# 16-bit tables for TensorE's register loads in a graph network kernel

## What is computed

```python
for l in range(3):
    X = einsum('ne,ref->rnf', out, weights[l])
    msg = X[edge_type, src] + biases[l][edge_type]
    hidden = segment_sum(msg, dest, N)      # dest = first row of edge_index
    out = relu(hidden) if l < 2 else hidden
x = layernorm(x + out)
# attention: alpha = cosine(x[row], x[col]) * beta, softmax over the edges of a row,
# out = segment_sum(alpha * x[col], row);   x = layernorm(x + out)
```

## Time and profile before

| | us |
|---|---|
| median of three runs | 5249.69 |
| the three runs | 5255.31, 5249.69, 5236.56 |
| span of the profiled execution | 4129.8 |
| PE busy | 2926.3 |
| DVE busy | 2722.0 |
| POOL busy | 2587.4 |

### The profile page before, as it was taken

The page is one execution under the profiler, slowest core; times in us unless marked ns, Lnnn a source line. Parts: engine busy times, 40 slices in busy tenths (PEclk is TensorE's granted clock), DMA queues, the critical chain, the costliest instruction groups (busy, mean ns, idle before and its releaser), DMA issues.

```text
span 4129.8 us, 59123 instructions
## 1 busy us (share of the span) xinstructions
PE 2926.3 (71%) x14075; PEld 1889.2 (46%) x14077; DVE 2722.0 (66%) x9148; ACT 820.3 (20%) x1995; POOL 2587.4 (63%) x2738
## 2 busy tenths in 40 slices
PE   7899966776777677676777667776766444446998
PEld 4455544444444444444444444444444333334776
DVE  9988875666666666666666656666665333336999
ACT  2588801001100100100100010000010000003665
POOL 0677767777777770777777777437777777771000
PEclk9899988888888888888888888888887555557999
DMA  4100013322332333332233233243224111113654
GB/s 154 51 2 2 6 41 78 85 74 73 86 78 73 82 80 150 77 85 74 73 86 78 72 82 82 53 180 81 73 73 91 53 53 53 53 53 100 191 187 142
DMA packets 373888, 336.56 MB, mean 81 GB/s; under 512 B 262034, under 2 KB 326090, under 8 KB 373448
## 3 DMA queue, kind: packets, MB, share of 16 engines
q0 software_dynamic: 87104, 158.80, 15.6%
q1 hardware_dynamic: 83112, 113.25, 8.1%
q10 hardware_dynamic: 203360, 60.73, 6.1%
HBM read 225.44 MB, written 107.13 MB: 81 GB/s over the span
## 4 chain that ended last, share of the span: by engine, by line
PE 36%; DVE 34%; issue 12%; POOL 11%; ACT 4%; DMA 2%; DVEq 0%; SPq 0%; POOLq 0%; ACTq 0%
PE ps L1067 12%; POOL region L935 11%; PE ps L1012 9%; DVE region L605 9%; DVE region L539 9%; DVE region L540 7%; PE ps L1056 7%; DVE oh L534 3%; PE ps L1128 2%; PE ps L1098 2%; PE ps L1156 2%; DMA region<-x_of_type,arrays 2%; ACT ps L1214 2%; ACT region L1225 2%; DVE region L378 1%
## 5 line engine op out<-in xcount | busy, mean ns | idle before, releaser
L935 POOL DMA_INDIRECT region<-x_of_type,arrays x2418 | 2286.8, 946 | 945.6 <-issue 718.3
L1067 PE MATMUL ps<-region 128*128 128x510 f16 x4200 | 1455.6, 437 | 551.2 <-issue 297.5
L534 DVE TENSOR_SCALAR oh<-iota_w,arrays 128x102 f32<-128x102 f32 x2528 | 734.2, 292 | 1303.9 <-PE ps L1056 1265.6
L1056 PE MATMUL ps<-region,oh 128*102 x5040 | 1142.9, 332 | 552.6 <-SPq L837 357.6
L1056 PEld LDWEIGHTS ps<-region,oh 128*102 128x102 f32 x5040 | 967.8, 212 | 1129.6 <-issue 870.8
L1067 PEld LDWEIGHTS ps<-region 128*128 128x128 f16 x4200 | 443.1, 108 | 665.6 <-issue 620.3
L605 DVE TENSOR_TENSOR region<-region,ps 102x128 f32 x2520 | 713.3, 283 | 3.4 <-issue 3.1
L1225 ACT COPY region<-ps 128x510 f32<-128x510 f32 x155 | 89.8, 579 | 2374.6 <-PE ps L1067 2374.2
L539 DVE TENSOR_SCALAR region<-ps,arrays 128x640 f16<-128x640 f16 x844 | 459.3, 544 | 0.0
L918 POOL DMA_INDIRECT scattered_edges<-region x304 | 296.5, 975 | 208.1 <-DVE shiftcol L442 110.4
L540 DVE TENSOR_SCALAR region<-ps,arrays 128x510 f16<-128x510 f16 x844 | 399.5, 473 | 0.0
(11 more groups left out here) (217 smaller groups left out, 1441.7 us busy)
## 6 DMA issues: line engine op xcount, KB each, us to landing
edge_counts<-region ACTq DMA_DIRECT2D x155, 255.0 KB
region<-x_of_type,arrays POOLq DMA_INDIRECT x2418, 2.5
arrays<-edge_counts SPq DMA_DIRECT2D x40, 960.0 KB, 5.0
x_of_type<-region SPq DMA_DIRECT2D x50, 576.0 KB, 2.8
edge_absent<-region ACTq DMA_DIRECT2D x155, 127.5 KB
region<-edge_absent SPq DMA_DIRECT2D x40, 480.0 KB, 4.0
x_of_type<-x0st SPq DMA_DIRECT2D x51, 192.0 KB, 1.8
scattered_edges<-region POOLq DMA_INDIRECT x304, 2.1
```

The lines of the kernel that those rows point to most:

```text
L534: ins = nc_.tensor_scalar(oh[:, t % U, 0:RB], iota_r, rowf[:, t % NT:t % NT + 1], None, ALU.is_equal)
L935: pool.indirect_dma_start(out=grow[:, t % GR * D:(t % GR + 1) * D], out_offset=None, in_=xt, in_offset=bass.IndirectOffsetOnAxis(ap=gix[:, ...
L1056: mm = pe.matmul(ps[0:RB, 6 + n % 2, t * D:(t + 1) * D], oh[:, u % U, 0:RB], grow[:, bass.ds(at[u % PAIRS], D)], start=True, stop=True)
L1067: mm = pe.matmul(ps[:, c, 0:CW], cl[:, q % CR, c * P:(c + 1) * P], cr[:, q % CR, :], start=False, stop=False, skip_group_check=True)
```

## The change

- The three tables are 16-bit integers without sign, all in `x0st`, in rows of ROW16 = 16 numbers (32 bytes). A row of `steps_of` belongs to PAIRS = 8 slots: 8 places (`slot_at`) and 2 due tiles (`tile_due`). A row of `banks_due` belongs to one turn's 10 cells and holds CG times (block number + 1), what was `b7`'s value plus CG - 1. `b7` is no longer used for it, nor is its padding set.
- PE loads a row of 8 + 2 numbers every 8 slots with one load (`steps_at`), where it had one load of 8 and one of 2.
- PE loads 10 bank numbers at the start of a turn with cells (`banks_at`), where it had two loads of 5 within the turn.
- Both declare why their values stay in bounds, so no comparisons and assertions follow.
- The wait for `s_cz` takes the register as it is, without adding CG - 1.

```diff
--- before.py
+++ after.py
@@ -22,6 +22,7 @@
 F16 = mybir.dt.float16
 I32 = mybir.dt.int32
 I16 = mybir.dt.int16
+U16 = mybir.dt.uint16
 ALU = mybir.AluOpType
 ACT = mybir.ActivationFunctionType
 AX = mybir.AxisListType
@@ -41,6 +42,7 @@
 KS = 14
 ROW_BIT = 15
 DIGIT = 11
+ROW16 = 16
 
 
 def gnn_program(nc, x, src, dst, edge_type, weights, biases, beta, out):
@@ -228,8 +230,13 @@
 
         ltri = oh[:, 0, :]
         shiftw = oh[:, 1, :]
-        spots = x0st[:, :, :].rearrange("p u w -> p (u w)").bitcast(I32)
-        slot_at, tile_due = spots[:, 0:NT], spots[:, NT:NT + NT // SLOTS]
+        spots = x0st[:, :, :].rearrange("p u w -> p (u w)").bitcast(U16)
+        steps_of = spots[:, 0:NT // PAIRS * ROW16].rearrange("p (k w) -> p k w", w=ROW16)
+        slot_at, tile_due = steps_of[:, :, 0:PAIRS], steps_of[:, :, PAIRS:PAIRS + PAIRS // SLOTS]
+        banks_due = spots[:, NT // PAIRS * ROW16:(NT // PAIRS + CTURNS) * ROW16].rearrange(
+            "p (k w) -> p k w", w=ROW16)[:, :, 0:CB]
+        assert PAIRS + PAIRS // SLOTS <= ROW16 and CB <= ROW16 and CQ == NT and HW % CB == 0
+        assert (NT // PAIRS + CTURNS) * ROW16 <= 2 * (X0 - 2) * G3
         spare = oh[:, 2:8, :].rearrange("p u d -> p (u d)")
         x0 = [x0st[:, q, :] for q in range(X0 - 2)] + [spare[:, 0:G3], spare[:, G3:2 * G3]]
         iota_r = iota_w[:, 0:RB]
@@ -316,11 +323,20 @@
                 blkt[0:1, bass.ds(k * SLOTS, SLOTS)], engines=[mybir.EngineType.DVE], min_val=0, max_val=(MB - 1) * D,
                 skip_runtime_bounds_check_because="blkt holds D times a group from 0 to MB - 1, made in this program")[1]
 
-        def slots_at(k):
+        def steps_at(k):
+
+            both = nc.values_load_multi_w_load_instructions(
+                steps_of[0:1, k, 0:PAIRS + PAIRS // SLOTS], engines=[mybir.EngineType.PE], min_val=0, max_val=(GR - 1) * D,
+                skip_runtime_bounds_check_because="steps_of holds D times a tile's number modulo GR, and tiles due from 1 "
+                                                  "to GT, made in this program as 16-bit numbers without a sign")[1]
+            return both[0:PAIRS], both[PAIRS:]
+
+        def banks_at(k):
 
             return nc.values_load_multi_w_load_instructions(
-                slot_at[0:1, bass.ds(k * PAIRS, PAIRS)], engines=[mybir.EngineType.PE], min_val=0, max_val=(GR - 1) * D,
-                skip_runtime_bounds_check_because="slot_at holds D times a tile's number modulo GR, made in this program")[1]
+                banks_due[0:1, k, :], engines=[mybir.EngineType.PE], min_val=0, max_val=CG * MB,
+                skip_runtime_bounds_check_because="banks_due holds CG times a group's number from 1 to MB, made in this "
+                                                  "program as 16-bit numbers without a sign")[1]
 
         def reg_wait(eng, s, value):
 
@@ -473,12 +489,13 @@
                 if k < 2:
                     nc_.tensor_scalar(blkt[:, halves(k)], ps[:, 5 + k, 0:HW], float(D), None, ALU.mult)
                 elif k < 4:
-                    nc_.tensor_scalar(b7[:, halves(k - 2)], ps[:, 3 + k, 0:HW], float(CG), 1.0, ALU.mult, ALU.add)
+                    rows = slice((k - 2) * (HW // CB), (k - 1) * (HW // CB))
+                    nc_.tensor_scalar(banks_due[:, rows, :], ps[:, 3 + k, 0:HW].rearrange("p (k q) -> p k q", q=CB),
+                                      float(CG), float(CG), ALU.mult, ALU.add)
                 elif k < 6:
                     step(nc_.tensor_tensor(tile[:, halves(k - 4)], iota_s[:, halves(k - 4)],
                                            ps[:, 4 + 3 * (k - 4), 0:HW], ALU.subtract))
                 elif k == 6:
-                    nc_.memset(b7[:, NT:KW], CG * (MB - 1) + 1)
                     nc_.tensor_tensor(tilecol[:, 0:TC - 1], number[:, 0:TC - 1], ps[:, 4, HW:HW + TC - 1], ALU.subtract)
                     step(nc_.tensor_tensor(tilecol[0:NT % P, TC - 1:TC], number[0:NT % P, TC - 1:TC],
                                            ps[0:NT % P, 4, HW + TC - 1:HW + TC], ALU.subtract))
@@ -492,10 +509,10 @@
                     step(nc_.scalar_tensor_tensor(out=lap, in0=lap, scalar=-float(GR), in1=tile_i,
                                                   op0=ALU.mult, op1=ALU.add))
                 elif k == 11:
-                    nc_.tensor_scalar(slot_at, lap, float(D), None, ALU.mult)
+                    nc_.tensor_scalar(slot_at, lap.rearrange("p (k u) -> p k u", u=PAIRS), float(D), None, ALU.mult)
                 elif k == 12:
-                    nc_.tensor_scalar(tile_due, tile_i.rearrange("p (k u) -> p k u", u=SLOTS)[:, :, SLOTS - 1], 1.0,
-                                      None, ALU.add)
+                    nc_.tensor_scalar(tile_due, tile_i.rearrange("p (k n u) -> p k n u", u=SLOTS, n=PAIRS // SLOTS)[:, :, :, SLOTS - 1],
+                                      1.0, None, ALU.add)
                 else:
                     c = k - 13
                     w = min(P, NT - P * c)
@@ -1047,8 +1064,9 @@
                 for u in range(BODY):
                     n, t = divmod(u, SLOTS)
                     if u % PAIRS == 0:
-                        at = slots_at((i * BODY + u) // PAIRS)
-                        due = values_of(pe, tile_due, (i * BODY + u) // PAIRS, GT, PAIRS // SLOTS, 1)
+                        at, due = steps_at((i * BODY + u) // PAIRS)
+                    if cells and u == 0:
+                        ready = banks_at(TURNS * l + i)
                     if t == 0:
                         reg_wait(pe, s_seq, due[u % PAIRS // SLOTS] + GT * l)
                         pe.wait_ge(s_oh, i * (BODY // SLOTS) + (first // SLOTS + n + 1))
@@ -1060,10 +1078,8 @@
                     for q, c in PARTS[u] if cells else ():
                         k = i * CB + (CB * TURNS * l + q)
                         if c == 0:
-                            if q % CR == 0:
-                                ready = values_of(pe, b7, k // CR, CG * (MB - 1) + 1, CR)
                             pe.wait_ge(s_co, k + 1)
-                            reg_wait(pe, s_cz, ready[q % CR] + (CG - 1))
+                            reg_wait(pe, s_cz, ready[q])
                         mm = pe.matmul(ps[:, c, 0:CW], cl[:, q % CR, c * P:(c + 1) * P], cr[:, q % CR, :],
                                        start=False, stop=False, skip_group_check=True)
                         if c == CG - 1:
```

## The result

The changed kernel takes 5212.48 us (median of 6, 5205.16 to 5227.11) where the kernel before, run beside it, takes 5249.74 (median of 6, 5236.56 to 5255.76): a ratio of 0.9923, 95% interval 0.9902 to 0.9944. That is 37.3 us less; 37 had been forecast.

The account below looks back on a forecast made before the run. POOL's gathers pace the layers, so a faster PE wins only the tails after the last gathers of layers 0 and 1: 21.6 + 18.7 = 40.3 us, less 1.5 us a layer, 37 us: 5213 us, range 5180 to 5250.

Parts of the forecast that it names:

- the gathers pace the layers: Layers: POOL's gather stream is fixed, 1008 and 1005 us in layers 0 and 1; PE never holds it back.
- The bank numbers were the stall: PE, before the cells' matmuls: bank loads and their pairs leave the array dry, 3.56 us a turn in layer 0.
- PE crosses from slower than POOL to faster: Layer 0: PE's turn goes from 29.4 to about 25.9 us, against POOL's 28.8.
- The tails: Last gather to first transposes, layers 0 and 1: 33.9 and 31.0 us become 12.3 each, 40.3 us saved.
- The rest at nothing: Table writes in the first stage, one memset less, DVE's and ACT's loads, earlier freed ring tiles: no gain or loss counted.
- The load's price: PE's new loads of ten 16-bit numbers: 0.6 us each, from 0.545 to 1.25 us, 1.87 at the longest.
- The rival with the price by pieces: PE's 16-bit loads fetch halfwords two at a time, 2.7 us a load: slower, about 5594 us; chance 0.07.
- Nothing new is exposed: Start of a turn: bank load and load of places take 1.2 us together, less than the 1.7 us before.
- The room: PE's turn can lose 2.9 us before PE is again behind POOL, 3.56 before it is as slow as before.
- The 1120 us outside the span: Median minus profiled span: taken to lie outside the span, so the saving counts once, 37 us.
- The rival of the hidden tail: Timed runs' gathers 0.46 us slower each, PE already caught up: no gain, 5240 to 5255; 0.18 with no effect.
- PE is the bound all through: Rival: PE at its lower clock, POOL waits; 84 turns give 3.56 us each, 299 us, about 4950; chance 0.07.

Follow-up runs that it names:

- e7: The kernel before with only the bank numbers as 16-bit rows of ten, one load at the start of a turn, no assertions: 4088.29 us, ratio 0.9893.
- e6: The kernel before with only tile places and due tiles as 16-bit rows, one load, no assertions; bank numbers stay in 32-bit loads of five: 4148.15 us, ratio 1.0043.
- e10: The changed kernel with the bank row loaded twice, 2.39 us more for PE's sequencer in each of 84 turns: ratio 1.0003 of before.
- e3: The changed kernel's layout and four loads a turn, but 32-bit numbers and one register operation on each waited-for value: 4087.2 us, ratio 0.9898 to before.
- e11: The changed kernel with the bank row and the middle steps' row of each turn loaded twice, 4.8 us more in a turn: 4242 us.
- e8: The changed kernel with each of the three steps' rows a turn loaded twice, 7.2 us of sequencer time more in each of 105 turns: near 4400 us.
- e4: The changed kernel with each steps' row of 8 + 2 sixteen-bit numbers loaded by two loads, 8 and 2: 4088.53 us, ratio 0.9901 to before.
- e5: The changed kernel itself, run again beside the kernel before, at the lower level: 4088.21 us, ratio 0.9892.
- e12: The kernel before, unchanged, run again for a trace at the upper level: 5255.09 us, ratio 1.0007.

## Why the prediction was right, point by point

Right: **the gathers pace the layers at the lower level**, 1005 to 1008 us with either kernel, and with 154 us less of PE's idle time before the cells of layer 0. **The bank numbers were the stall**: e7 gives the whole gain and e6 none. Their "issue" is gone from before the cells; the share forecast, 3.56 us a turn, was on the low side, since all idle time there fell by 154 / 35 = 4.4 us a turn. **PE crosses from slower than POOL to faster**: in layer 0 it runs 1.7 us behind the arrivals where it ran 15.0 behind, and waits some 94 us for gathers. **The tails**: 12.8 and 11.4 us for 12.3 each; 40.7 us saved for 40.3. The rest at nothing: the first gather starts 0.4 us later, the way between layers is 2.7 and 1.2 us shorter, the end 1.1 longer. The 1.5 us a layer taken off for a late block end didn't show.

**The load's price, wrong by four**: 2.39 us for 0.6, and outside the bounds of 0.545 to 1.87. The step that failed is "the closest in length and place": 32 bytes at an aligned address is what the two loads share, but the price of 16-bit numbers goes by their count. A row on record had that price: the slow form of five numbers, 1245 ns, is 249 ns a number, and would be 2.5 us for ten; the sum took it as a price of the load, 1.25 us. The rival with the price by pieces had this right, 2.7 us a load against 2.39 measured, and its time, 5594 us, wrong by 380, since all of it rests on four loads counted in full on a turn of 25.9 us. PE's own turn with loads of 2.39 us in it is 26.2 us, and 25.9 had been forecast with loads of 0.6. So two errors offset each other. "Nothing new is exposed" at the start of a turn was wrong, 2.2 us of idle time a turn are new there; and what was removed before the cells had cost 4.4 us a turn where the idle time booked on it was 3.56. In the stream of the kernel before the steps' loads hide for the most part: by e6 three of them a turn, 0.7 us longer each than the loads and pairs that they replace, leave the last cells' matmuls of layer 0 at 1574.23, where they were at 1574.22, and cost 17 us in all, where counted in full they would make 2.05 x 70 = 143 in layers 0 and 1.

**The room**: 2.9 us a turn until PE is again behind POOL, and 3.56 until the kernel is as slow as before. With 26.2 us a turn it is 2.6 for the first. For the second, e10 says 2.4: an added 2.4 us a turn brings 1.0003 of before. This term was mis-sized by a third.

**The 1120 us outside the span, wrong**: 2 us lie outside it. They are a level of the execution, in the first stage (352 us until the first gather), in the gathers (224, 238 and 193 us in the three layers of before) and in the three tails (119 us together). The rival of the hidden tail put them into slower gathers, 0.46 us more each. The gathers start 0.28 us further apart (1232 / 805 = 1.53 us), but they are not slower, POOL waits between them, and the tail is not hidden: at 79.7 us it is longer than at the lower level. The rival "PE is the bound all through" has POOL held back by PE, which is what the starts of the gathers look like at this level, and its 299 us are wrong, because the idle time taken from PE before the cells came back before the slots. That the forecast's 5213 us met 5212.48 is thus in part luck: the mechanism it rests on, read at the lower level, gives 43 us there and only about half of the saving at the level of the median, and the rest comes from the pace of the gathers in layers 1 and 2, where the forecast had nothing.

## What to carry to other kernels

A sequencer's register work counts where the engine's array runs dry behind it: look for "issue" before the instructions that follow a load, and look at what is checked behind it before shortening the load itself. Then look for the time at its new place: here 154 us of idle time before the cells went, and 76 came back at the start of the turns. A releaser that counts up steadily gets the blame for every long stop behind it; whether it was really waited for is told by when its work was done. Where another engine paces a loop, a faster stream is worth only the backlog at the loop's end, read as the distance from the pacer's last instruction to the first that needs all sums; once that backlog is gone, a cheaper load brings nothing (e3), and a dearer one costs in full as soon as it eats the room (e10, e11, e8). And compare the span of the profiled execution with the median first: if they differ by a quarter, as here, the trace is of another kind of execution than the timed runs, and its waits need not be theirs.

## What the runs showed of the hardware

Register loads on PE's queue, medians: two 32-bit numbers 545 ns, eight 592 ns, ten 1079 ns at rows 48 bytes apart; at rows 40 bytes apart 1077 and 2422 ns in turn (e3); five at rows 20 bytes apart 590 ns for every fourth load and 1247 for the others (before); two 16-bit numbers 514 ns, eight 1921 ns (e4), ten 2390 ns (e5). In these loads a 16-bit number costs 235 ns, so that packing numbers to halfwords makes a load of ten 2.2 times as long as that of 32-bit numbers in rows on a 16-byte boundary, and no longer than that of 32-bit numbers off it.

The same program runs at 4130 or at 5250 us. At the upper level PE does 160 matmuls in 350 us of the first stage instead of 1859, at a granted clock of 0.51 instead of 0.98, its matmuls 2.80 us apart. Its profiles hold about a third of the semaphore events of the others (23109 and 22336 in e12 and after, 64595 and 64610 in before and e5), and releasers "remote" for 333.4 us of POOL's waits. What causes the level stayed open; that the recording itself has to do with it is a rival that no run tested.
